# Two mixture-of-experts layers: all experts for all tokens, or 39 sorted tiles of chosen tokens with row gathers ahead of row scatters

## What is computed

```python
m = _layernorm(x, ln2_g, ln2_b)
xt = m.reshape(-1, Dd)
probs = jax.nn.softmax(xt @ Wg, axis=-1)
wts, idx = jax.lax.top_k(probs, K)                       # K = 2 of E = 8
wts = wts / jnp.sum(wts, axis=-1, keepdims=True)
h1 = jax.nn.gelu(jnp.einsum('td,edf->etf', xt, W1) + b1[:, None, :])   # 128 -> 512
ye = jnp.einsum('etf,efd->etd', h1, W2) + b2[:, None, :]               # 512 -> 128
sel = ye[idx, jnp.arange(T)[:, None], :]
moe_out = jnp.sum(wts[..., None] * sel, axis=1)
return x + moe_out
```

## Time and profile before

| | us |
|---|---|
| median of 3 runs | 3081.71 |
| profiled execution, its own time | 3089.07 |
| its span, first to last instruction | 3087.4 |
| PE busy in it | 2811.2 |
| DVE busy | 2016.6 |
| ACT busy | 1746.3 |
| POOL busy | 260.1 |

### The profile page before, as it was taken

One profiled execution on the slowest core, in us unless ns is written; L12 is line 12 of the kernel. 1 busy time (PEld: TensorE's weight loads), 2 busy tenths in 40 slices (PEclk: granted clock), 3 DMA queues, 4 the chain that ended last, 5 costly groups with the idle time before them and its releaser, 6 DMA issues. The chain is left out here.

```text
span 3087.4 us, 50997 instructions
## 1 busy us (share of the span) xinstructions
PE 2811.2 (91%) x15207; PEld 1321.3 (43%) x15207; DVE 2016.6 (65%) x2997; ACT 1746.3 (57%) x3339; POOL 260.1 (8%) x488
## 2 busy tenths in 40 slices
PE   6788856999999999899599999949999999998998
PEld 2688853433333333444244444424333333334443
DVE  5544457788888883322478888747888888872222
ACT  4222211677777787443236776722877777775443
POOL 1222202000000000000111111220000000000000
PEclk9888855899999999899779999966999999998999
DMA  1000002110111100111111111020110111100111
GB/s 39 1 0 0 0 1 75 29 28 17 25 28 28 28 19 3 63 62 41 62 37 35 40 41 41 22 75 14 29 26 17 27 28 28 27 8 14 69 61 34
DMA packets 37080, 94.16 MB, mean 31 GB/s; under 512 B 9258, under 2 KB 23044, under 8 KB 28804
## 3 DMA queue, kind: packets, MB, share of 16 engines
q1 hardware_dynamic: 33892, 91.18, 10.9%
q10 hardware_dynamic: 3104, 1.88, 0.2%
HBM read 78.45 MB, written 13.76 MB: 30 GB/s over the span
## 5 line engine op out<-in xcount | busy, mean ns | idle before, releaser
L509 DVE TENSOR_REDUCE Fmaxes<-Fm 128x1 f32<-128x1024 f32 x512 | 603.4, 1220 | 100.4 <-PE Fm L273 98.9
L509 DVE TENSOR_REDUCE Hmaxes<-Hm 128x1 f32<-128x1024 f32 x512 | 603.4, 1220 | 99.2 <-PE Hm L273 97.7
L420 ACT ACTIVATE Fprob<-Fs 128x512 f32<-128x512 f32 x1024 | 528.5, 604 | 118.1 <-PE Fs L285 117.6
L420 ACT ACTIVATE Hprob<-Hs 128x512 f32<-128x512 f32 x1024 | 528.5, 604 | 117.9 <-PE Hs L285 117.4
L285 PE MATMUL Fs<-Fqa,Fka 64*128 64x512 f32 x1024 | 409.2, 466 | 5.8 <-ACT Fprob L420 5.2
L285 PE MATMUL Hs<-Hqa,Hka 64*128 64x512 f32 x1024 | 409.0, 466 | 5.9 <-ACT Hprob L420 5.4
L905 ACT ACTIVATE Lprob<-Ls 128x512 f32<-128x512 f32 (+3 forms) x640 | 301.7, 542 | 127.3 <-PE Ls L786 126.5
L273 PE MATMUL Fm<-Fka,Fqa 64*128 64x512 f32 x1024 | 350.4, 460 | 19.6 <-DMA Fka<-F_kparts 15.9
L273 PE MATMUL Hm<-Hka,Hqa 64*128 64x512 f32 x1024 | 350.2, 460 | 18.6 <-DMA Hka<-H_kparts 14.9
L273 PEld LDWEIGHTS Fm<-Fka,Fqa 64*128 64x128 f32 x1024 | 162.1, 195 | 277.1 <-DVE Fmaxes L509 252.9
L273 PEld LDWEIGHTS Hm<-Hka,Hqa 64*128 64x128 f32 x1024 | 161.9, 195 | 275.9 <-DVE Hmaxes L509 253.0
(11 more groups left out here) (448 smaller groups left out, 2997.3 us busy)
## 6 DMA issues: line engine op xcount, KB each, us to landing
Fqa<-F_qparts SPq DMA_DIRECT2D x64, 128.0 KB
Fka<-F_kparts SPq DMA_DIRECT2D x64, 128.0 KB
FEwb<-FE_weights SPq DMA_DIRECT2D x8, 1024.0 KB, 5.8
Lqa<-L_qparts SPq DMA_DIRECT2D x64, 128.0 KB
Lka<-L_kparts SPq DMA_DIRECT2D x64, 128.0 KB
Hqa<-H_qparts SPq DMA_DIRECT2D x64, 128.0 KB
Hka<-H_kparts SPq DMA_DIRECT2D x64, 128.0 KB
HEwb<-HE_weights SPq DMA_DIRECT2D x8, 1024.0 KB, 5.5
```

The source lines that it names most:

```text
L420: nc.scalar.activation(prob[:, kt % PSLOTS, q0:q1], seat(kt, n)[:, 0:q1 - q0], ACT.Exp, scale=SCALE).then_inc(expd, 1)
L509: nc.vector.reduce_max(maxes[:, qt, half:half + 1], mps[j % 2][:, 0:width], AX.X)\
```

## The change

Both calls of `experts` and `project_add` give way to one stage, `experts_sorted`, that computes an expert only for the tokens that chose it. The 4096 pairs of token and choice are put in order by expert, every expert's list padded to whole tiles of 128. However the tokens choose, that needs at most 39 tiles (TILES, 32 + 8 - 1), and all 39 are always computed.

- **Routing and tables.** After the two largest are found, DVE counts pairs for each expert (`chosen`, `upto`, with three small matmuls on PE, L1365 to L1368), gives each pair a place in the order (`place`, `pos`), and forms one-hot tensors of 32 x 39 and 32 x 128 elements a partition (`tile`, `pair`, `rank`, L1488 to L1499). 32 matmuls (L1373) turn these into a table: for each tile and partition the token and its weight (`rows`, `wtab`). `owner` is the expert of a tile, `ownint` the same as integers, `b1s` the bias for each tile.
- **Stores and loads.** SP stores the normalized tokens in DRAM (`m_d`, 1 MB), loads all of W2 (2 MB) and 16 small copies of b2. For each tile it reads the expert's number from SBUF to a register (L1285) and loads that expert's W1 (256 KB) into one of 4 slots (L1288).
- **Output bias and residual.** POOL adds `n1` to `x` (L1304); PE makes the weighted b2 with four matmuls of 512 columns (L1380), and DVE adds these to `x` (L1529).
- **The tiles.** POOL gathers the 128 rows of each tile with an indirect DMA (L1310), all 39 of them first, at most 4 in flight. PE transposes a tile (`turn`, L1337), DVE applies gain and bias (L1536), PE makes 4 products of 128 columns (L1346), ACT four gelus of 128 columns (L1408), PE 4 more products (L1355), whose W2 address comes from a register read at the head of each step (L1389), and DVE scales the result (L1545). Behind the last gather in POOL's program stand the 39 scatters (L1319), each an indirect DMA that writes the 128 result rows to DRAM by pair number, again at most 4 in flight.
- **The end.** When all scatters have landed, SP loads the 4096 rows back in 8 DMAs of 256 KB (L1293), and DVE adds them to `x` in 8 instructions.

```diff
-def experts(nc, name, mT, wg, w1_d, b1T, w2_d, b2T, accT, consts):
...
+TILES = 2 * NT + E_N - 1
+SPARE = 2 * T
+KEEP = 4
...
+def experts_sorted(nc, name, m, mT, wg, w1_d, b1T, w2_d, b2_d, gain, bias, x, n1, consts, moves, turn_no):
...
+            @block.sync
+            def _(sp):
+                sp.dma_start(m_d.rearrange("(t p) c -> p t c", p=P), m[:, :, :]).then_inc(kept, 16)
+                sp.dma_start(w2[:, :, :], w2_d.rearrange("e (k p) c -> p (e k) c", p=P)).then_inc(w2_in, 16)
+                sp.wait_ge(filled, FILLED)
+                for t in range(NT):
+                    sp.dma_start(b2s[t * E_N:(t + 1) * E_N, t // 4, t % 4, :], b2_d).then_inc(b2_in, 16)
+                sp.wait_ge(step, at["own"])
+                for k in range(TILES):
+                    s = k % KEEP
+                    e = sp.value_load(ownint[0:1, 0, k:k + 1], min_val=0, max_val=E_N - 1)
+                    if k >= KEEP:
+                        sp.wait_ge(up, k - KEEP + 1)
+                    sp.dma_start(w1[:, s, :], w1_d[bass.ds(e, 1), :, :].rearrange("o c f -> (o c) f")).then_inc(w1_in[s], 16)
+                for s in range(KEEP):
+                    sp.wait_ge(y_out[s], moved_at(s, len(range(s, TILES, KEEP))))
+                for b in range(NB):
+                    for j in range(TOP):
+                        sp.dma_start(back[:, j, 4 * b:4 * b + 4, :],
+                                     y_d[j * T + b * BANK:j * T + (b + 1) * BANK, :].rearrange("(t p) c -> p t c", p=P))\
+                            .then_inc(back_in[b], 16)
...
+                nc.gpsimd.tensor_tensor(x[:, :, :], x[:, :, :], n1[:, :, :], ALU.add).then_inc(filled, 1)
+
+                def gather(k):
+                    s = k % KEEP
+                    if k >= KEEP:
+                        pool.wait_ge(x_in[s], moved_at(s, k // KEEP))
+                    nc.gpsimd.indirect_dma_start(xs[:, k, :], None, m_d[:, :],
+                                                 bass.IndirectOffsetOnAxis(rows[:, 1, k:k + 1].bitcast(U32), 0))\
+                        .then_inc(x_in[s], 16)
+
+                def scatter(k):
+                    s = k % KEEP
+                    pool.wait_ge(scaled, k + 1)
+                    if k >= KEEP:
+                        pool.wait_ge(y_out[s], moved_at(s, k // KEEP))
+                    nc.gpsimd.indirect_dma_start(y_d[:, :],
+                                                 bass.IndirectOffsetOnAxis(rows[:, 0, k:k + 1].bitcast(U32), 0),
+                                                 ys[:, k, :], None).then_inc(y_out[s], 16)
+
+                pool.wait_ge(kept, 16)
+                pool.wait_ge(step, at["tokens"])
+                for k in range(TILES):
+                    gather(k)
+                for k in range(TILES):
+                    scatter(k)
...
+                def turn(k):
+                    s = k % KEEP
+                    pe.wait_ge(x_in[s], moved_at(s, k // KEEP + 1))
+                    if k >= 2:
+                        pe.wait_ge(taken, k - 1)
+                    nc.tensor.transpose(xps[k % 2][:, 0:P], xs[:, k, :], consts["ident"]).then_inc(turned, 1)
+
+                def raise_(k):
+                    s = k % KEEP
+                    pe.wait_ge(w1_in[s], 16 * (k // KEEP + 1))
+                    pe.wait_ge(taken, k + 1)
+                    if k >= 3:
+                        pe.wait_ge(gelu, (k - 2) * FC)
+                    for f in range(FC):
+                        last = nc.tensor.matmul(hps[k % 3][:, f * P:(f + 1) * P], w1[:, s, f * P:(f + 1) * P],
+                                                xg[:, k % 2, :], start=True, stop=True)
+                    last.then_inc(up, 1)
+
+                def lower(k, e):
+                    if k >= 2:
+                        pe.wait_ge(scaled, k - 1)
+                    for f in range(FC):
+                        pe.wait_ge(gelu, k * FC + f + 1)
+                        last = nc.tensor.matmul(yps[k % 2][:, 0:C], hid[:, k % 2, f, :],
+                                                w2[:, :, :].rearrange("p k c -> p (k c)")[:, bass.ds(e + f * C, C)],
+                                                start=(f == 0), stop=(f == FC - 1))
+                    last.then_inc(down, 1)
...
+                pe.wait_ge(step, at["pair1"])
+                for q in range(NB):
+                    pe.wait_ge(step, at["rank", q])
+                    for n in range(q * 8, q * 8 + 8):
+                        last = nc.tensor.matmul(tps, rank[:, n, :], pair[:, n, :, :], start=(n == 0), stop=(n == 2 * NT - 1))
+                last.then_inc(tabled, 1)
+                pe.wait_ge(step, at["wts"])
+                nc.tensor.transpose(wps, wts[:, :, :].rearrange("p t e -> p (t e)"), consts["ident"]).then_inc(wt, 1)
+                pe.wait_ge(b2_in, 16 * NT)
+                pe.wait_ge(wt_sb, 1)
+                for b in range(NB):
+                    nc.tensor.matmul(b2ps[b][:, :], wT[:, :], b2s[:, b, :, :].rearrange("p t c -> p (t c)"),
+                                     start=True, stop=True).then_inc(b2_made, 1)
+                pe.wait_ge(step, at["b1s"])
+                turn(0)
+                turn(1)
+                pe.wait_ge(b2_added, NB)
+                pe.wait_ge(w2_in, 16)
+                raise_(0)
+                for k in range(TILES):
+                    e = pe.value_load(ownint[0:1, 1, k:k + 1], min_val=0, max_val=(E_N - 1) * FC * C)
+                    if k + 1 < TILES:
+                        raise_(k + 1)
+                    if k + 2 < TILES:
+                        turn(k + 2)
+                    lower(k, e)
...
+                act.wait_ge(step, at["b1s"])
+                for k in range(TILES):
+                    if k >= 2:
+                        act.wait_ge(down, k - 1)
+                    act.wait_ge(up, k + 1)
+                    for f in range(FC):
+                        nc.scalar.activation(hid[:, k % 2, f, :], hps[k % 3][:, f * P:(f + 1) * P], ACT.Gelu_apprx_tanh,
+                                             bias=b1s[:, k, f:f + 1]).then_inc(gelu, 1)
...
+                nc.vector.tensor_tensor(tile[:, :, :], count(TILES), wide(ab[:, 0, :], TILES), ALU.is_equal)\
+                    .then_inc(step, 1)
+                need("tile")
+                nc.vector.tensor_tensor(pair[:, :, 0, :], tile[:, :, :], wide(val[:, :], TILES), ALU.mult).then_inc(step, 1)
+                nc.vector.tensor_tensor(pair[:, :, 1, :], tile[:, :, :],
+                                        wide(wj[:, :, :].rearrange("p j t -> p (j t)"), TILES), ALU.mult).then_inc(step, 1)
+                for q in range(NB):
+                    n = slice(q * 8, q * 8 + 8)
+                    nc.vector.tensor_tensor(rank[:, n, :], consts["count"].unsqueeze(1).broadcast_to([P, 8, P]),
+                                            ab[:, 1, n].unsqueeze(2).broadcast_to([P, 8, P]), ALU.is_equal)\
+                        .then_inc(step, 1)
+                tiles_e = [P, TILES, E_N]
...
+                dve.wait_ge(tabled, 1)
+                nc.vector.tensor_tensor(rows[:, 0, :], consts["spare"], tps[:, 0, :], ALU.subtract).then_inc(step, 1)
+                need("rows")
+                nc.vector.tensor_scalar(rows[:, 1, :], rows[:, 0, :], T - 1, None, ALU.bitwise_and).then_inc(step, 1)
+                nc.vector.tensor_copy(wtab[:, :], tps[:, 1, :]).then_inc(step, 1)
...
+                for b in range(NB):
+                    dve.wait_ge(b2_made, b + 1)
+                    nc.vector.tensor_tensor(x[:, 4 * b:4 * b + 4, :], b2ps[b][:, :].rearrange("p (t c) -> p t c", t=4),
+                                            x[:, 4 * b:4 * b + 4, :], ALU.add).then_inc(b2_added, 1)
+
+                def take(k):
+                    dve.wait_ge(turned, k + 1)
+                    if k >= 2:
+                        dve.wait_ge(up, k - 1)
+                    nc.vector.tensor_scalar(xg[:, k % 2, :], xps[k % 2][:, 0:P], gain, bias, ALU.mult, ALU.add)\
+                        .then_inc(taken, 1)
+
+                take(0)
+                take(1)
+                for k in range(TILES):
+                    if k + 2 < TILES:
+                        take(k + 2)
+                    dve.wait_ge(down, k + 1)
+                    nc.vector.tensor_scalar(ys[:, k, :], yps[k % 2][:, 0:C], wtab[:, k:k + 1], None, ALU.mult)\
+                        .then_inc(scaled, 1)
+                dve.wait_ge(b2_added, NB)
+                for b in range(NB):
+                    dve.wait_ge(back_in[b], 16 * TOP)
+                    for j in range(TOP):
+                        if j:
+                            dve.wait_ge(added, b * TOP + j)
+                        nc.vector.tensor_tensor(x[:, 4 * b:4 * b + 4, :], x[:, 4 * b:4 * b + 4, :],
...
 def build(nc, a, table, out):
...
-            experts(nc, name + "E", main, G["Wg"], ffn_in["W1"], col["b1"], ffn_in["W2"], col["b2"], yT, consts)
-            project_add(nc, name + "X", yT, None, x, x, consts, also=n1)
```

(43 more changed lines are left out.)

286 lines of the change are left out of this document (159 added, 127 removed).

## The result

The changed kernel takes **2915.34 us** (median of 4 runs, 2914.59 to 2915.91) against 3082.06 us for the kernel before beside it: ratio 0.9455, 95% interval 0.9438 to 0.9472. The saving of 166.7 us lies between the forecast's 183 us and the 101 us of the first rival at c = 1.8.

A forecast was written before the change was run, and what follows sets the result against it. The prediction took PE's columns to bound the expert stage. Setup 40, tiles 89.7 and end 14.9 made 144.6 us against 236.3, saving 183 us over two stages: 2899 us from 3081.7, range 2860 to 3025.

The forecast's parts named there:

- the first rival: Expert stage: POOL's queue of 78 indirect DMAs sets the end; 2981 us at c = 1.8; chance 0.22.
- c: Time one indirect DMA holds POOL, taken as 1.2 us; above 1.25 us POOL sets the stage's end.
- PE sets the end: Expert stage: PE finishes at 129.7 us, POOL's scatters at 125.6, so PE decides by 4 us; chance 0.56.
- the rival's formula: Stage length if POOL sets the end: 32 + 78c + 2.1 + 9.9 + 1.4 = 45.4 + 78c us.
- A tile: Tile loop on PE: 1.99 us of records and transpose plus 0.3 for the register read, 2.3 us; 39 make 89.7.
- Setup: Stage start to tile 0's first product: 40 us, bounds 36 and 45; POOL's gathers start at 32.
- An indirect DMA: POOL's gathers and scatters of 128 rows: 1.2 us each, between 0.25 and 2.9.
- The end: Stage's tail: scaling 0.3, last scatter's issue 1.2 and landing 2.1, read-back 9.9, additions 1.4, together 14.9 us.
- Slow clock in the loop: Tile loop: gaps get PE 1.2 GHz, a tile takes about 3.9 us, the program 3023 us; chance 0.08.
- One at a time: POOL's queue: each indirect DMA holds it until landed, 2.1 us each, the program 3023 us; chance 0.06.
- Slower: POOL's queue: from c = 2.45 us on it outlasts PE's former columns, up to 3152 us; chance 0.06.
- no change: Whole program: c within a few hundredths of 2.45 us, time within 0.3%, 9 us; chance 0.02.

The follow-up runs named there:

- Experiment 7: Changed kernel plus eight 512-column products that nothing reads on PE ahead of the table matmuls: 2906.31 us, ratio 0.9421 to the kernel before.
- experiment 5: Changed kernel with gathers of 64 rows instead of 128, the other half of each tile a constant: 2914.66 us, ratio 0.9448 to the kernel before.
- experiment 6: Changed kernel with DVE's owned, spread and b1s moved ahead of its wait for the table: 2917.05 us, ratio 0.9451 to the kernel before.

## Why the prediction was right, and where not

The size was right to 16 us in 2915, and the engine named was wrong. **The step that failed is "PE sets the end".** It is the first rival's mechanism that ran, just past its limit: the limit was c = 1.25 us, and 78 indirect DMAs took (1399.1 - 1298.6) / 78 = 1.29 us each. By the rival's formula, 45.4 + 78 x 1.29 = 146 us; with the setup's delay of 7.8 it is 153.8, and 153.0 was measured.

That 2899 came so near is in part luck. A tile was 0.40 us too dear, 15.6 us in all. That made the sum by PE 5.6 us a stage longer than the sum by POOL, and so hid 5.6 of the 14.6 us by which the start (7.8) and the queue (6.8) were too cheap. With the tile at 1.90 and all else as forecast, POOL would have set the end in the prediction's own sum, with 139.0 us a stage and 2887 us for the program, 28 us short. So it was the 0.3 us for the register read that chose the engine. The three sizes that decided it:

*Setup, 40 us forecast, first gather 7.8 us late.* The chain of small instructions was right: logits at 7.0 us (5.9), table begun at 24.6 (23.9). The table was sized 7.5 to 11.7 us from records at 0.62 clock and at full clock, and I took 7.7. It took 13.9, above my upper bound: the granted clock was 0.50, not 0.62. The mistake was to take the fast end for an engine that the same paragraph says has nothing to do before. Experiment 7 shows the other case, 7.3 us, so the price was right for a PE at the high clock. The b2 products took 6.7 us instead of 3.6, in a stretch with a granted clock of 0.62. PE's first hidden product came at 46.8 us, where 40 was forecast with 45 as the upper bound.

*A tile, 2.3 us forecast, 1.90 measured.* The read takes 0.30 us, as taken, but none of it was on PE's path: it runs under the products still in PE's queue, and PE is busy 73.2 of 74.4 us. Columns, gelu (368 ns against 366), clock 1.00 and weights four tiles ahead were as forecast. The prediction saw that cover, 0.94 us of output products, and still put the read on top. The Trainium skill (DMA: Bandwidth & Descriptors, Latency and other measured facts) has a floor near 600 ns for a tensor_load; the trace has 268 ns on SP and 300 on PE, and here the measurement decides. The estimate of 2.0 us a tile that the prediction worked out from that figure was the better one all the same.

*An indirect DMA, 1.2 us forecast, 1.25 and 1.28 measured*, and 3.38 for the first. The guess from POOL's rate by size was near in sum but not in its make: rows cost 44 ns for 64, and the rest is fixed (experiment 5). These three together shift PE's end from +129.7 to +122.7 and POOL's from +125.6 to +140.2, and so turn 4 us of slack on POOL into 17.5 us on PE.

*The end* was forecast at 13.4 us behind the last scatter and took 12.8. *The sum*: by POOL's queue the forecast had 32 + 93.6 + 13.4 = 139.0 us, 5.6 less than by PE. Measured are 39.8 + 100.4 + 12.8 = 153.0. The 8.4 us over the forecast's 144.6 are 7.8 for the late start and 6.8 for the queue (2.2 of them the first gather), less 0.6 at the end and less the 5.6 by which PE was to come after POOL.

*The rivals.* Slow clock in the loop: no, 1.00. One at a time: no; the gathers are 1.25 us apart with four slots. The Trainium skill (DMA: Bandwidth & Descriptors, Anatomy of one DMA) has some 2.0 us fixed for each DMA of this path, mostly waiting for completion. This trace agrees as far as it can say: POOL stood no longer than its own 0.30 us in front of any scatter, so four in flight did not hold it. Slower and no change: no, c was far from 2.45. The signs that the prediction named for the first rival, scatters back to back behind the last product with SP waiting for them, are what the trace shows. Of the signs for its being right only the clock held: the gathers were over at 90.5 us instead of 80, the table ended at 38.5 instead of 32, and the last scatter came 17 us behind the last scaling, not within 2.

Two questions stay open. Why `spread` takes 2.38 us, where three other products and comparisons of 1248 elements take 1.45 to 1.46, was not tried; in experiment 6 POOL was idle beside it, so POOL is not the reason. The code sets it apart: it reads the bias columns in steps of four elements. A second instruction points the same way, the product at L1464, which reads `place` in steps of 16 elements and takes 590 ns for 256 elements, where two others of 256 take 426 and 415 (L1437, L1509). No run tested it. And why the full DMA engines move 253 GB/s in the read-back, and not more, was not taken apart.

## What to carry to other kernels

When two engines' forecasts lie 4 us apart in 145, name the pair as the bound and price what each loses by a late start; here the common start (a table on the path at the low clock) cost more than the choice between them. Count a queue's instructions by a fixed price each before thinking of rows: an indirect DMA cost POOL 1.20 us with 64 rows and 1.25 with 128, so what helps is to have fewer of them (without the scatters a stage was 17 us shorter from its first gather on), and their order matters only where the queue would run empty. A few products that nothing reads in front of a short stretch of matmuls on the path took the table from 13.9 to 7.3 us, and that version, 2906 us, beats both kernels; with the bias chain early it is 2903 us, within the interval of the same.

## What the runs showed of the hardware

**An indirect DMA waited for a DVE product of two SBUF tensors.** The first gather started at 1298.64 beside `spread` (1298.29 to 1300.67) and ended at 1301.72, 1.05 us after it, which is one gather's own 0.95 and 0.1. Experiment 7's timeline has the same 1.06 us, from 1296.92 to 1297.98:

```profile
1294.50 2.42 DVE L1524 TENSOR_TENSOR FEspread<-FEowned,cols 128x1248 f32<-128x1248 f32 x1
...
1294.86 3.12 POOL L1310 DMA_INDIRECT FExs<-FE_tokens,FErows  x1 [25.20 <-DVE FEowned L1521]
```

With `spread` out of the way (experiment 6) it took 1.16 and 1.02 us. The Trainium skill (SBUF — State Buffer, SBUF: two separate sides) says that DVE and GpSimd share a pair of ports under an exclusive lock. By the Trainium skill (SBUF — State Buffer, A bandwidth-pool intuition that's wrong) the blocked one goes on about 115 ns after DVE's end, and the 0.1 us here agree. For a DVE instruction with two SBUF inputs the Trainium skill (SBUF — State Buffer, Who interferes with whom) has the lock bite only against a GpSimd instruction that reads SBUF. An indirect DMA's list of rows lies there (`rows`), so this case may be one of those, but no run here tells reads from writes. In the same section the Trainium skill says that its own probe saw no `tensor_tensor` stall a DMA; here one did, by 2 us, and the measurement decides. The later gathers ran beside DVE instructions with at most one SBUF input and were not held.

**The period of indirect DMAs**: 947 ns + 0.30 us for gathers, 972 ns + 0.30 us for scatters, 903 ns + 0.30 us for gathers of 64 rows, and 968 ns (gathers) and 987 ns (scatters) when they take turns.

**The granted clock of a short stretch follows what PE did before it.** With PE waiting for DVE ahead of the table it was 0.50 for the whole 14.1 us, though PE was busy all of that stretch. With eight products in front it was 1.00 from the table's start.
